# Other places in the issue order of a differential attention stage, in a two-layer decoder on one NeuronCore

## What is computed

```python
# per batch b (4), 16 heads of width 16, T = 256; h = layernorm(x)
q, k = h @ W_q_slots, h @ W_k_slots          # a head's two halves side by side, in 32 rows
q = q * lam_col                              # the second half is weighted with -lambda
s = q_head @ k_head.T                        # (256, 256)
p = exp((s - max(s, -1)) * 8 ** -0.5)
o = (p @ v_head) / p.sum(-1)
x = x + (o @ W_proj) * (1 - LAMBDA_INIT)
```

## Time and profile before

| | us |
|---|---|
| median of 3 runs (lowest, highest) | 1831.59 (1826.9, 1843.16) |
| the profiled execution | 1826.9 |
| its span, first to last instruction | 1825.0 |
| PE busy in the span | 1649.1 (90%) |
| DVE busy | 1279.3 (70%) |
| ACT busy | 855.8 (47%) |
| POOL busy | 558.6 (31%) |

### The profile page before, as it was taken

How to read it: one execution, slowest core, us unless ns; L and a number is a source line. 1 busy time by engine, 2 the same in 40 slices (tenths; PEclk the granted TensorE clock), 3 DMA queues, 4 the chain that set the end, 5 groups by cost and what they waited for, 6 DMA issues and landing times.

```text
span 1825.0 us, 51399 instructions
## 1 busy us (share of the span) xinstructions
PE 1649.1 (90%) x21686; PEld 1161.5 (64%) x21686; DVE 1279.3 (70%) x2850; ACT 855.8 (47%) x1404; POOL 558.6 (31%) x951
## 2 busy tenths in 40 slices
PE   5999999999867899899899889998988898899988
PEld 4899999998653455465466545664554455566557
DVE  6778777877577787877888353444367687888844
ACT  3343434433350465656666712442343466567652
POOL 5553544534142130501502031441021222431230
PEclk9999999999988999999999989998999999999999
DMA  3000100110008364262362383653812245554100
GB/s 127 23 25 1 47 13 13 53 43 1 20 10 172 56 132 98 47 152 51 84 119 49 70 322 111 226 185 101 160 24 40 46 82 133 87 106 77 24 2 24
DMA packets 91857, 143.94 MB, mean 79 GB/s; under 512 B 14870, under 2 KB 60123, under 8 KB 91628
## 3 DMA queue, kind: packets, MB, share of 16 engines
q1 hardware_dynamic: 87228, 127.79, 30.1%
q10 hardware_dynamic: 2528, 7.74, 1.3%
q0 software_dynamic: 1872, 5.13, 0.7%
HBM read 109.68 MB, written 32.03 MB: 78 GB/s over the span
## 4 chain that ended last, share of the span: by engine, by line
PE 67%; DVE 18%; ACT 5%; issue 5%; POOL 2%; DMA 1%; SPq 1%; DVEq 0%; ACTq 0%; POOLq 0%
PE bank L1076 17%; PE bank L1284 6%; PE bank L2029 6%; DVE shared L1357 4%; PE bank L1915 4%; PE bank L1917 3%; PE bank L1916 3%; PE bank L808 3%; PE bank L2048 3%; DVE xa_part_max L1357 3%; PE bank L2476 2%; ACT xa_e L1318 2%; PE bank L773 2%; PE bank L747 1%; PE bank L2491 1%
## 5 line engine op out<-in xcount | busy, mean ns | idle before, releaser
L1357 DVE TENSOR_REDUCE xa_part_max<-bank 128x1 f32<-128x448 f32 (+1 forms) x512 | 266.0, 567 | 22.3 <-PE bank L1076 20.3
L1318 ACT ACTIVATE xa_e<-bank 128x1024 f32<-128x1024 f32 (+1 forms) x208 | 212.2, 1024 | 124.6 <-PE bank L1076 122.5
L1318 ACT ACTIVATE ca_e<-bank 128x1024 f32<-128x1024 f32 (+2 forms) x208 | 197.4, 958 | 78.0 <-PE bank L1076 75.6
L1357 DVE TENSOR_REDUCE shared<-bank 128x1 f32<-128x400 f32 (+1 forms) x384 | 205.0, 569 | 29.2 <-PE bank L1076 25.8
L1076 PE MATMUL bank<-xa_kst,xa_qst 122*32 122x448 bf16 (+1 forms) x2048 | 182.5, 351 | 17.3 <-DVE xa_part_max L1357 9.7
L1284 PE MATMUL bank<-xa_e,xa_vaug 128*17 128x256 f32 (+1 forms) x1664 | 134.3, 381 | 6.8 <-ACT xa_e L1318 4.3
L1076 PE MATMUL bank<-xa_qst,xa_kst 128*32 128x256 bf16 (+1 forms) x3264 | 135.2, 274 | 1.3 <-DMA xa_qst<-xa_negT 1.3
L1284 PE MATMUL bank<-ca_e,ca_vaug 128*17 128x256 f32 (+2 forms) x1664 | 125.4, 373 | 3.6 <-ACT ca_e L1318 2.5
L1012 POOL TENSOR_TENSOR gsa_qk<-gsa_qk,gsa_rot 128x512 f32<-128x512 f32 x64 | 81.8, 1279 | 142.3 <-DVE gsa_rot L928 142.3
L1076 PE MATMUL bank<-xa_wkv,shared 128*32 128x256 f32 (+1 forms) x1632 | 112.6, 386 | 11.2 <-issue 4.4
L1076 PEld LDWEIGHTS bank<-xa_qst,xa_kst 128*32 128x32 bf16 (+1 forms) x3264 | 93.1, 97 | 31.8 <-issue 3.4
(11 more groups left out here) (408 smaller groups left out, 4181.0 us busy)
## 6 DMA issues: line engine op xcount, KB each, us to landing
xa_kst<-xa_k_parts SPq DMA_DIRECT2D x96, 200.1 KB, 5.0
ca_kst<-ca_k_parts SPq DMA_DIRECT2D x96, 200.1 KB, 5.2
xa_k_parts<-xa_parts SPq DMA_DIRECT2D x24, 400.2 KB, 4.7
ca_k_parts<-moe_ctx_parts SPq DMA_DIRECT2D x8, 1200.8 KB
moe_gu<-in_expert_gate_up SPq DMA_DIRECT2D x8, 1024.0 KB
shared<-in_ctxT_split ACTq DMA_DIRECT2D x4, 1601.0 KB, 8.7
moe_ctxT<-in_ctxT SPq DMA_DIRECT2D x8, 800.5 KB, 8.1
ca_cv<-in_ctx SPq DMA_DIRECT2D x4, 1536.0 KB
```

Source lines behind the costliest of these rows:

```text
L1318: e.activation(self.e[m % 3][0:rows, :, first:T], banks[m % 2][0:rows].rearrange("p a (h t) -> p (a h) t", t=T)[:, :, first:T], ACT.Exp, s ...
L1357: e.tensor_reduce(top, work[:, 0:hi - lo], AX.X, ALU.max).then_inc(*reduced(t, *step))
```

## The change

It gives other places to the steps of stage 4; no instruction is added or taken away, and no line outside `da_steps` is touched.

```diff
-            parts = [spread(norms, -19, -12.8), spread(project(0), -18.9, -8.8), spread(project(BANK), -1.3, 2), [(2.6, ("ahead", 0))]]
-            parts += [[(n * 4 - 3 + 1.9, ("ahead", n))] for n in range(1, B)]
+            parts = [spread(norms, -19, -8), spread(project(0), -19, -4), spread(project(BANK), 0.3, 5.3), [(0.3, ("ahead", 0))]]
+            parts += [[(n * 4 - 3 + 0.9, ("ahead", n))] for n in range(1, B)]
             for n in range(N_DA):
-                parts.append([(n - 1.9, ("top", n, 0)), (n - 1.1, ("top", n, 1)), (n - 0.4, ("fold", n)), (n, ("exp", n)),
-                              (n + 0.2, ("pv", n)), (n + 0.2, ("acc", n)), (n + 2.1, ("fin", n))])
+                parts.append([(n - 1.9, ("top", n, 0)), (n - 1.4, ("top", n, 1)), (n - 0.6, ("fold", n)), (n, ("exp", n)),
+                              (n + 1.3, ("pv", n)), (n + 1.3, ("acc", n)), (n + 2.5, ("fin", n))])
                 if n % UNITS == UNITS - 1 and n + 1 < N_DA:
-                    parts.append(added(n // UNITS, n + 2.4, 0.4))
+                    parts.append(added(n // UNITS, n + 3.2, 1))
                     if n + UNITS + 1 < N_DA:
-                        parts.append(queries_of(n // UNITS, n + 3.1, 0.9))
+                        parts.append(queries_of(n // UNITS, n + 4.3, 1))
             first = [("max", 0, h_, i, c) for h_ in range(UNIT) for i in range(TB) for c in range(len(ca_chunks))]
-            parts.append([(9.4, ("load", 0)), *spread(first, 10.5, 15.2), (15.7, ("neg", 0)), (15.7, ("neg_parts", 0)), (10.9, ("load", 1)), (19.7, ("neg_turn", 0))])
+            parts.append([(9.7, ("load", 0)), *spread(first, 10.9, 14.6), (14.6, ("neg", 0)), (14.6, ("neg_parts", 0)), (14.7, ("load", 1)), (15.3, ("neg_turn", 0))])
```

## The result

| | before | changed |
|---|---|---|
| median in us (lowest, highest), 4 runs each | 1837.4 (1826.9, 1855.8) | 1860.5 (1851.2, 1874.1) |
| profiled execution, its span | 1826.9, 1825.0 | 1852.7, 1850.6 |
| first top to stage 5's first scores | 130.9 | 158.1 |
| mean granted clock of the span | 0.972 | 0.958 |

The ratio is 1.0158, 95% interval 1.0115 to 1.0202: slower, by 21 to 37 us. The forecast was 1842, with 1854 as the end of its range. A fourth execution (1855.8) has moved the median of before from 1831.6 to 1837.4, so part of the distance between 1842 and 1860.5 is before's own scatter; measured against before, 10.4 us were forecast and 23.1 came.

What follows compares the result with a forecast made beforehand. PE was taken as the bound (67% of the chain, DVE 18%), all cost being waits: 4.2 + 3.6 + 7.7 - 2.1 - 0.8 = 12.6 us on 1826.9 gives 1839.5; with half of 4.7 added, 1842, range 1829 to 1854.

Steps and rivals of the forecast that it cites:

- Clock: At stage 5's start: work lost to the lower clock was 1.6 us; whether it stays up is even, so 0.8 off.
- The forecast of 13.4: Whole of stage 4: the changed order's lag of 13.4 us after the end's gain, before 0.8 off for clock.
- Start: First tops stand back to back, 2.53 us apart, with waits of 1.5, 1.5, 1.1 and 0.6, 4.6 us in all.
- the walk: Stage 4's new order placed step by step on the old durations, with in-order queues and waits for banks; exp 5 at 51.6.
- the clock falls at the start: Rival, at the first tops: half clock there costs 5 us, time 1847; chance 0.25.
- Up to exp 11: Exp 5 to exp 11: units take 5.48 us against 5.27, single steps wait 1.1 each; lag grows from 4.2 to 7.8.
- Up to exp 15: Exp 11 to exp 15: denser max steps make it 40.8 us against 33.1, 7.7 more; lag 15.5.
- the 7.7 us: Exp 11 to exp 15: the added time, 1.4 of four max steps put off and 6.1 of waits.
- End: Exp 15 to stage 5: 7.1 us instead of 9.15 by an earlier copy and DMA of the maxima; gain 2.1.
- The faster case: Rival, stage 4: late pv and early neg_turn remove waits and tops make none, 5.9 us gained, 1823; chance 0.08.
- ring: PE's banks in stage 4: a step waits for the bank taken three takes earlier; tops needing it start 2.53 us apart.
- The range: Whole kernel: 1829 to 1854 us, one in ten left out on each side; clock and denser waits reach 1854.

Runs made afterwards that it cites:

- fill_half: Changed kernel with fill_all's dummies, but 2 instead of 4 behind a top and 1 instead of 2 ahead of a first top; ratio 1.0124.
- fill_all: Changed kernel plus dummy float32 identity matmuls on PE, at the start and at the later waits; ratio 1.0112.
- max_back_fill: fill_all with the line of the maxima back at its old places; ratio 1.0136.
- units_outs: Kernel before with only the new offsets inside a unit and the new places of added and queries_of; ratio 1.0166.
- better: Kernel before with neg_turn moved from 19.7 to 15.8 and pv and acc from n + 0.2 to n + 1.2; ratio 0.9981.
- better_few: better plus dummy matmuls: 8 at the wait of 1.6 us, 1 and 2 before tops of the part with the maxima; ratio 0.9965.
- neg_early: Kernel before with only neg_turn moved from 19.7 to 15.8; ratio 0.9981.
- better_fill: better plus dummy matmuls: 1 before a unit's first top, 8 at the 1.6 us wait, 3, 4 and 2 before later tops and pv; ratio 1.0014.
- after_again: The changed kernel as it is, run once more for a second trace; ratio 1.0130.
- max_only: Kernel before with only the changed line of the maxima (load, max, neg, neg_turn); ratio 1.0008.

## Why the prediction was wrong

**The failed step is "Clock".** It set the clock at full in the whole stage and gave it a term at stage 5's start alone, -0.8. That the same fall could come at the start was named as a rival, but added nothing to the sum. The runs showed four stretches at half clock in the changed kernel, the same in two executions, with 20.7 us of lost work. With work in the waits, the stage was 10.6 us shorter; as the dummies also take time, 10.6 is the least the clock costs, and 20.7 the most. The change's 27.2 us are thus 10.6 to 20.7 of clock and 16.6 to 6.5 of order. The forecast of 13.4 (before its clock term) lies inside the part of the order, though not for its reasons, as the next paragraphs say.

**Start: right, with a rival's clock on top.** The waits are 1.56 and 1.38 for 1.5 and 1.5, exp 5 comes 52.7 us after the first top at full clock, 51.6 in the walk. In the changed kernel it is 57.0. The rival "the clock falls at the start" had 5 us for that, and 4.4 were measured. The Trainium skill, TensorE: Matmul & The Clock Gate, section "A second HAM failure mode: psum-queue depth-cycling", tells of a kernel that went through PSUM banks, idled shortly between its groups and swung between the two clocks. The trace agrees with it in all four stretches; I had applied it at one place. It would not have told the two orders apart by itself: the kernel before idles between its groups too, 3.6 us in ten waits, and kept 1.00 through the stage. What I held against the rival, PE busy 3.9 of 9.15 us at clock 1.00 after exp 15, was misread: that stretch ends in a fall of its own, to 0.63 and 0.52 right behind it. It was no evidence of a clock that holds.

**Up to exp 11: right order, size open.** The walk had 44.9 us, measured were 46.7 with 3.4 of lost work, and 46.6 in `fill_half` at full clock. At full clock without dummies it lies between 43.3 and 46.6. The wait of pv is gone, and single steps pay up to 1.1 us, as forecast.

**Up to exp 15: the size near, the reason wrong.** Walk 40.8; measured 47.6, of it 11.5 lost; at full clock between 36.1 and 40.8 (`fill_all`). I had put the 7.7 us on the denser maxima (as 1.4 and 6.1, which make 7.5). Alone they cost 0 to 3.7; with the maxima back at their old places (`max_back_fill`) the segment was 42.3. That `fill_all` took 40.8, the very figure of the walk, is luck. The long part comes from the new offsets of units, outs and queries: `units_outs` has 44.5 there. What in it makes the waits (the later outs, the later queries or the tops 0.3 closer to each other) was not separated: outs back alone can't be built, since `out_turn` would stand ahead of the `fin` that it needs.

**End: right.** 6.78 for 7.1, the wait for the DMA 1.24, and the clock stayed up there in both traces, a gain of the whole 1.6 us where I had taken half. `better` and `better_few`, which change the pv and `neg_turn` in before's start and units, show 7.69; `neg_early`, without the late pv, 8.52: the two edits are needed together.

**The faster case** was said to need shorter reductions or a looser ring. For the places of the change nothing shows otherwise, but another order needed neither: with before's tops and the pv a unit late, units up to exp 5 lost 1.4 us of waits, the end 1.4; and in `better_few` dummies kept the clock. A late pv and an early `neg_turn` were in the change too, along with offsets that undid their gain; the dummies were not.

**The range.** Its upper end took in the clock at the start and some more waits. It left out that a pattern that pulls the clock down at one place of the stage stands at three more.

## What to carry to other kernels

Where an order adds short waits on the engine of the matmuls, cost them twice, as waits and as the work of that whole stretch at half clock, if the trace of before shows anywhere a similar pattern at 0.50. Whether the clock will fall these runs could not foretell; take the two costs as the ends of a range. Dummy matmuls in the waits tell in one run how much of the loss is clock at the least; too many turn the engine into the bound (in `better_fill` PE was busy 35.8 of 37.0 us between exp 11 and exp 15), so vary their number. And when a change moves several groups of steps, run each alone before you blame the one whose density looks worst.

## What the runs showed of the hardware

The clock is not set by one wait. The kernel before has a wait of 1.62 us that ends at 1359.41, PE busy 0.59 of 2 us there, and its clock stayed at 1.00. `better` has the same wait, 1.62 us, and the clock fell right behind it. First the window of before, then two of `better`:

```profile
1358.00:1360.00 2.00, 0.59 (x6) 0.54 (x8) 1.76 (x5) 0.79 (x1) 1.16 (x1) 1.00 0.00 0
```

```profile
1354.00:1356.00 2.00, 0.70 (x6) 0.20 (x2) 1.97 (x4) 1.70 (x2) 1.63 (x2) 1.00 0.00 0
1356.00:1358.00 2.00, 1.68 (x16) 0.94 (x20) 1.07 (x4) 0.00 (x0) 0.32 (x1) 0.81 0.34 95
```

What differs between them I can't say; both had short waits of 0.16 to 0.34 us in the units ahead.

The same holds at the end of the stage. From exp 15 on `better` and `better_few` have the same matmuls with the same waits (1.06, 0.64 and 1.15 us in one, 1.05, 0.64 and 1.16 in the other), at clock 1.00 in both. The first two us of stage 5, first of `better`, then of `better_few`:

```profile
1425.31:1427.31 2.00, 2.00 (x36) 1.51 (x40) 0.62 (x2) 1.03 (x1) 0.00 (x0) 0.55 0.65 145
```

```profile
1414.43:1416.43 2.00, 2.00 (x52) 1.40 (x56) 1.06 (x3) 1.33 (x2) 0.00 (x0) 1.00 0.68 136
```

The low level lasts. In the changed kernel it held from 1401 to 1422 us:

```profile
1401.00:1422.00 21.00, 17.50 (x122) 7.79 (x120) 11.00 (x24) 3.05 (x5) 3.58 (x8) 0.52 0.00 1
```

PE's rows say busy 17.5 of 21 us, which looks like a full engine. It is the work of about half that time at 2.4 GHz, stretched. A busy share has to be read with the clock of the same window.

Ahead of 1288 us, nearly all of it in stages that no kernel here touches, 27.8 to 40.1 us were lost to the clock in the traces here, and the first top lies between 1283.7 and 1303.5. The trace with the earliest first top (`after_again`) lost the least there, and the one with the latest (`max_only`) the most: this scatter of 20 us is of the same size as the effect of the change.
